# Attention with pairs weighted between scores and transposes, inverse sums spread by matmuls, and other steps for VectorE's copies

## What is computed

```python
q = _split_heads(query_antecedent @ Wq, h) * d_head ** (-0.5)
k = _split_heads(memory_antecedent @ Wk, h)
v = _split_heads(memory_antecedent @ Wv, h)
logits = jnp.einsum('bhqd,bhkd->bhqk', q, k) + bias
weights = jax.nn.softmax(logits, axis=-1)
x = jnp.einsum('bhqk,bhkd->bhqd', weights, v)
b, _, l, d = x.shape
x = x.transpose(0, 2, 1, 3).reshape(b, l, h * d)
return x @ Wo
```

## Time and profile before

| | us |
|---|---|
| median of the timed runs | 1054.37 |
| profiled execution | 1050.43 |
| its span, first to last instruction | 1048.7 |
| PE busy | 985.9 (94%) |
| VectorE busy | 611.1 (58%) |
| ScalarE busy | 484.5 (46%) |
| GpSimd busy | 261.3 (25%) |

### The profile page before, as it was taken

How to read it: one execution, slowest core, us unless ns; L and a number is a source line. 1 busy time by engine, 2 the same in 40 slices (tenths; PEclk the granted TensorE clock), 3 DMA queues, 4 the chain that set the end, 5 groups by cost and what they waited for, 6 DMA issues and landing times.

```text
span 1048.7 us, 17978 instructions
## 1 busy us (share of the span) xinstructions
PE 985.9 (94%) x7218; PEld 798.9 (76%) x7218; DVE 611.1 (58%) x1209; ACT 484.5 (46%) x625; POOL 261.3 (25%) x223
## 2 busy tenths in 40 slices
PE   7899999999999999999999999768869999999995
PEld 6588777888777888777887777343459999989884
DVE  4335986465986466986454984588961112455551
ACT  3111786062786155786151786368711102455551
POOL 0401840001840001840001830588310101111100
PEclk9999999999999999999999999898959999999998
DMA  8182871522871614871421853700059949699930
GB/s 281 40 156 76 191 185 47 203 81 75 192 180 47 264 40 151 191 175 50 150 106 37 195 124 122 283 1 2 23 189 389 377 164 342 206 381 334 329 91 13
DMA packets 76923, 169.91 MB, mean 162 GB/s; under 512 B 6440, under 2 KB 16808, under 8 KB 71968
## 3 DMA queue, kind: packets, MB, share of 16 engines
q1 hardware_dynamic: 74720, 163.87, 51.0%
q0 software_dynamic: 2112, 4.80, 2.0%
HBM read 119.01 MB, written 16.10 MB: 129 GB/s over the span
## 4 chain that ended last, share of the span: by engine, by line
PE 78%; DMA 6%; DVE 6%; POOL 4%; issue 3%; ACT 2%; SPq 1%; POOLq 0%; DVEq 0%; ACTq 0%
PE psum L461 11%; PE psum L2117 9%; PE psum L441 7%; PE psum L476 7%; PE psum L2132 6%; PE psum L380 5%; PE psum L397 5%; PE psum L398 5%; PE psum L399 5%; PE psum L381 5%; PE psum L382 5%; DMA xg<-xm_rows,row_id 3%; PE psum L2149 2%; PE psum L2151 2%; PE psum L2150 2%
## 5 line engine op out<-in xcount | busy, mean ns | idle before, releaser
L883 POOL CAST stack<-kT 128x2048 fp32r<-128x2048 f32 x32 | 64.0, 2006 | 405.3 <-DVE keys_lo L592 393.6
L628 DVE CUSTOM_DVE_ANT_0 prob<-psum,biasmap,top 128x512 f32<-128x512 f32 x192 | 144.2, 751 | 21.4 <-PE psum L441 12.0
L796 ACT ACTIVATE prob<-prob,top 128x2048 f32<-128x2048 f32 x64 | 128.5, 2008 | 27.0 <-DVE top L628 26.6
L461 PE MATMUL psum<-ident,prob 128*128 128x128 f32 x1024 | 134.9, 275 | 1.2 <-issue 0.8
L2117 PE MATMUL psum<-xT,wring 128*128 128x128 f32 (+3 forms) x1024 | 135.1, 293 | 0.6 <-ACT xT L2430 0.6
L2117 PEld LDWEIGHTS psum<-xT,wring 128*128 128x128 f32 x1024 | 132.7, 193 | 1.5 <-ACT xT L2430 0.8
L461 PEld LDWEIGHTS psum<-ident,prob 128*128 128x128 f32 x1024 | 116.3, 141 | 22.1 <-issue 7.5
L758 ACT COPY kT<-psum 128x512 f32<-128x512 f32 x64 | 37.5, 586 | 198.7 <-PE psum L382 191.7
L804 ACT COPY probT<-psum 128x1024 f32<-128x1024 f32 x96 | 96.5, 1010 | 45.6 <-PE psum L476 44.0
L397 PE MATMUL psum<-wv_hi,ctx_part 128*128 128x512 f32 x256 | 100.1, 391 | 0.0
L398 PE MATMUL psum<-wv_lo,ctx_part 128*128 128x512 f32 x256 | 99.8, 390 | 0.0
(11 more groups left out here) (256 smaller groups left out, 1721.1 us busy)
## 6 DMA issues: line engine op xcount, KB each, us to landing
wring<-in_w SPq DMA_DIRECT2D x64, 1024.0 KB, 7.8
ctx_raw<-in_ctx_t SPq DMA_DIRECT2D x15, 1024.0 KB, 6.0
stack<-stack SPq DMA_DIRECT2D x32, 256.0 KB, 4.7
early_stack<-early_stack SPq DMA_DIRECT2D x28, 256.0 KB, 5.2
ternary<-ternary_weights SPq DMA_DIRECT2D x1, 6272.0 KB, 24.7
prob<-in_w_gate_t SPq DMA_DIRECT2D x1, 5632.0 KB, 17.4
stack<-key_stack SPq DMA_DIRECT2D x20, 256.0 KB, 3.9
query_stacks<-prob SPq DMA_DIRECT2D x16, 256.0 KB, 5.4
```

What stands on the lines that cost most here:

```text
L461: mm = pe.transpose(psum[:, w + i, j * P:(j + 1) * P], prob[:, prob_slot(n, j), kt * P:(kt + 1) * P], ident[:, :])
L628: dve.tensor_tensor_reduce(prob[:, slot, keys], psum[:, scores.of[n, j, c], :], biasmap[:, keys], 1.0, top[:, h, (c + 1) % 2:(c + 1) % 2 + ...
L796: act.activation(prob[:, slot, :], prob[:, slot, :], ACT.Exp, bias=top[:, h, 1:2], scale=-1.0, accum_out=top[:, h, 2:3]).then_inc(*raised. ...
```

## The change

- In a slot, and in the tail, PE weighs the older pair first, then turns the sums where they are due, and then turns the newer pair. The first of these stood last before.
- The spread copy goes. `turn_sums` makes four matmuls, one for each head, with that head's column of `rinv` repeated 32 times as the weights and the identity as the moving operand; each writes its 32 rows of the bank. It waits for the reciprocal (`inverted`). `copy_sums` now has the wait for the `finish` before it, and the reciprocal a wait for the sums turned two quads before.
- VectorE's pairs are 2 and 6 where they were 3 and 7, and 2, 6 and 7 in the third quad where they were 3, 6 and 7.
- `finish` of the quad before the last stands between the two bias additions of slot 3; it stood behind both.

```diff
-MOVED_BY_VECTOR = ((3, 7), (3, 7), (3, 6, 7), (7,))
+MOVED_BY_VECTOR = ((2, 6), (2, 6), (2, 6, 7), (7,))
...
             def turn_sums(n):
                 w, free = scores.take(("sums", n), sums_copied.at(n))
-                pe.wait_ge(*spread_out.at(n))
+                pe.wait_ge(*inverted.at(n))
                 pe.wait_ge(*free)
-                pe.transpose(psum[:, w, 0:P], inverse[:, :], ident[:, :]).then_inc(*sums_turned.made(n))
-
-            def turn_and_weigh(b, turned_step, weighed_step):
+                for j in range(QUAD):
+                    mm = pe.matmul(psum[j * DH:(j + 1) * DH, w, 0:P], rinv[:, n % 2, j:j + 1].broadcast_to([P, DH]),
+                                   ident[:, :], start=True, stop=True, tile_position=(0, j * DH))
+                mm.then_inc(*sums_turned.made(n))
+
+            def weigh_and_turn(b, turned_step, weighed_step, summed):
+                if weighed_step is not None:
+                    multiply_pair(*pair_of_step(b, weighed_step))
+                if summed is not None:
+                    turn_sums(summed)
                 if turned_step is not None:
                     turn_pair(*pair_of_step(b, turned_step))
-                if weighed_step is not None:
-                    multiply_pair(*pair_of_step(b, weighed_step))
...
-            def spread_sums(n):
+            def invert_sums(n):
                 g = n % DT
                 dve.wait_ge(*raised.at(n, QUAD - 1))
-                dve.reciprocal(rinv[:, n % 2, :], top[:, QUAD * g:QUAD * (g + 1), 2]).then_inc(*own.made())
-                dve.wait_ge(*own.last())
+                if n >= 2:
+                    dve.wait_ge(*sums_turned.at(n - 2))
+                dve.reciprocal(rinv[:, n % 2, :], top[:, QUAD * g:QUAD * (g + 1), 2]).then_inc(*inverted.made(n))
+
+            def copy_sums(n):
+                dve.wait_ge(*sums_turned.at(n))
                 if n >= 1:
                     dve.wait_ge(*weighted.at(n - 1))
-                dve.tensor_copy(inverse[:, :].rearrange("p (j d) -> p j d", j=QUAD),
-                                rinv[:, n % 2, :].rearrange("p (j d) -> p j d", d=1).broadcast_to([P, QUAD, DH])
-                                ).then_inc(*spread_out.made(n))
-
-            def copy_sums(n):
-                dve.wait_ge(*sums_turned.at(n))
                 dve.tensor_copy(inverse[:, :], psum[:, scores.of["sums", n], 0:P]).then_inc(*sums_copied.made(n))
...
-                        for c in (2 * half, 2 * half + 1):
-                            add_bias(n, j, c)
+                        add_bias(n, j, 2 * half)
+                        if i == FINISH_AT and n > DT * b + 1:
+                            finish(n - 2)
+                        add_bias(n, j, 2 * half + 1)
                         step = steps_of_slot(n, i)[0] if n > DT * b else None
                         if step is not None and by_vector(*pair_of_step(b, step)):
                             move_pair(*pair_of_step(b, step))
-                        if i == 3 and n > DT * b + 1:
-                            finish(n - 2)
-                        if i == 3 and n > DT * b:
-                            spread_sums(n - 1)
+                        if i == INVERT_AT and n > DT * b:
+                            invert_sums(n - 1)
                         if i == SUMS_AT and n > DT * b:
                             copy_sums(n - 1)
```

More of the change, by code:

```diff
@@ L56 @@
 FILLERS = (2, 1, 2, 1, 2, 1, 2, 1, 2, 2)
-SUMS_AT = 5
+FINISH_AT, INVERT_AT, SUMS_AT = 3, 3, 5
 class Events:
@@ L290, in perceiver_block @@
         moved_a = events("moved_a", [(n, p) for n, p in pairs if not by_vector(n, p)])
-        spread_out = events("spread_out", quads)
-        sums_turned, sums_copied = events("sums_turned", quads), events("sums_copied", quads)
+        inverted, sums_turned, sums_copied = (events(name, quads) for name in ("inverted", "sums_turned", "sums_copied"))
         weighted = events("weighted", quads)
@@ L539, in tensor_attention @@
                         if n > DT * b:
-                            turn_and_weigh(b, *steps_of_slot(n, i))
-                        if n > DT * b and i == SUMS_AT:
-                            turn_sums(n - 1)
+                            weigh_and_turn(b, *steps_of_slot(n, i), n - 1 if i == SUMS_AT else None)
                 work.restart()
                 for t in TAIL:
-                    turn_and_weigh(b, t, t - WEIGH_LATER)
-                    if t == STEPS - 3:
-                        turn_sums(DT * (b + 1) - 1)
+                    weigh_and_turn(b, t, t - WEIGH_LATER, DT * (b + 1) - 1 if t == STEPS - 3 else None)
                 multiply_pair(*pair_of_step(b, STEPS - 2))
@@ L742, in vector_attention @@
                 finish(last - 1)
-                spread_sums(last)
+                invert_sums(last)
                 if b + 1 < B:
```

## The result

The changed kernel takes 1061.71 us (median of 10 runs, 1057.32 to 1065.23), the kernel before beside it 1054.03 (10 runs): ratio 1.0069, 95% interval 1.0051 to 1.0087, some 7.7 us more. The forecast was 1060.7 us and +6.3.

The account below looks back on a forecast made before the run. The prediction took PE to bound the attention slots. Its terms, -3.3 + 2.1 + 7.7 + 0.5 - 0.7 = +6.3 us, carried over to the timed median of 1054.37 gave 1060.7 us, own range 1057.5 to 1063.5.

Parts of the forecast that it names:

- The bound: Attention stage: PE's blocks follow without a gap, 2.11 us a slot, so only PE's blocks or waits count.
- Order: Attention slots on PE: scores (S) 0.63, weighting (W) 0.58, transposes (T) 0.85; slot 2.06 instead of 2.11 us, -3.3 us.
- Sums by matmuls: Inverse sums on PE: four matmuls, 0.22 us, replace one transpose; +2.1 us over the kernel.
- VectorE's steps: VectorE in attention: dropping the spread copy and moving `finish` and other waits costs or saves PE nothing, 0 us.
- Copies: VectorE's copy of pair 2 before slot 5's additions stalls slot 6's second score matmul 0.64 us, 12 times: +7.7 us.
- The 0.5 us for slot 2: Copy of pair 6 behind slot 0 delays slot 2's second score matmul by 0.06 us in 8 places: +0.5 us.
- the small gains: Shorter wait for ScalarE's first copy in quad 1's slot 4, and no last-exponential wait in the tail: -0.7 us together.
- A: Score ring: PE hides the stall, being held elsewhere by as much; 1055 us, or 1053.0 with no stall; chance 0.18.
- B: PE's attention slots: cheaper junctions between blocks give a slot of 1.92 us and a total of 1049.5 us; chance 0.12.
- C: PE's attention: first, the order saves nothing, 1064.0 us; second, the repeated column loads slowly, 1066.5; chance 0.12 for both.

## Why the prediction was right

Point by point, by its own steps.
- **The bound.** PE without a gap in the slots: right. Each edit showed up in the attention stretches through PE's blocks or PE's waits.
- **Order.** S 0.63, W 0.58, T 0.85, slot 2.06: measured 0.64 to 0.65, 0.57 to 0.58, 0.85, 2.07. Prices read from rows with the same neighbours carried over. Against the kernel before, the blocks S and T of the slots give 2.1 us, where I had 3.3: the 0.015 us by which S is longer than I took stand there some 80 times. The tail, which I put at nothing, takes 0.5 of it back: the order before ended in two weightings in a row, 1.01 us, and in the new order a turn stands between them and they take 0.57 or 0.58 each. The Trainium skill ("TensorEngine Tiling", Key Properties) says only that a change of tiling mode drains TensorE. Read as one price for every change, which is how I set it against my rows, it gives a slot of 2.11; the slot of 2.07 is against that reading, by 0.04 us a slot.
- **Sums by matmuls.** +2.1 us forecast, 2.0 to 2.1 measured in the blocks of the kernel with them alone, and 2.4 in the changed kernel, where the turn behind the sums lasts 0.88, 0.03 more than I took. In the changed kernel, though, this term isn't there to be added: PE would have waited for the same bank without it, as the run with the old transpose showed.
- **VectorE's steps.** 0 forecast, and no wait for `finish` and none behind pair 7 shows in the changed kernel. The order alone shows what the two edits kept away: 1.4 us and 4.4 us.
- **Copies.** Twelve stalls of 0.64 forecast, 7.7 us; twelve of 0.49 measured, 5.9 us. The mechanism was right and the size too large, by two latencies. A turn in front of S frees VectorE 0.28 us after the next slot starts (305.53 against 305.25), not 0.37; and PE's matmul starts 0.06 us after the bank is read out (308.27 against 308.21), not 0.17. PE also reaches the slot 0.04 later, after 2.32 us and not 2.28. The other way, the W behind a late matmul starts 0.43 after it (308.27 to 308.70), not 0.31. The 0.5 us for slot 2 weren't there: with the 0.28 the additions are in time.
- **The sum.** +6.3 forecast, +6.46 in the stretches, +7.7 in the medians. That the first two agree so well is luck in good part, as the copy terms were 2.3 too large together and the order 1.2 too favourable. The blocks of both timelines, one by one, divide the 6.46 so: stalls +5.9; sums +2.4; order in the slots -2.1; quad 1's slot 4 -0.7, where the turn behind ScalarE's first copy takes 0.85 for 1.02 (this and 0.2 in the tail are the small gains that I put at 0.7); a wait of 0.23 us that only before's trace has, -0.2; the tails without the sums +0.8, mainly the 0.5 just named, less 0.2, and 0.4 in the last batch with its wait for a DMA; the projections of quad 0 and of the first slots of quad 1 +0.3. Together +6.4. What makes the medians differ by 1.2 us more than the stretches isn't settled; the interval of the ratio (+5.4 to +9.2 us) takes in both.
- **Rivals.** A (hidden stall) is refuted by the twelve S of 1.13. B (cheaper junctions) is refuted by the blocks. C's first half is refuted by the slot of 2.07, its second by 0.22 to 0.25 us for the sums.
- **The range.** 1061.71 lies in the prediction's own range, 1057.5 to 1063.5. Its sentence that the range takes in A's 1053 and C's 1064.5 doesn't go with that range, and C's own sum was 1064.0.

What the prediction got right by its sum it described badly in one respect: it treated the parts as additive. The three parts alone cost 5.2 (order), 2.4 (matmuls) and 6.5 (copies) us of stretches, 14.1 together; the change, which is these three and the new place of `finish` (it has no run of its own), costs 6.5. The waits of the order alone go with pairs 3 and 7 and with the old place of `finish`, and the stall of the copies hides the matmuls.

## What to carry to other kernels

Where two engines hand banks round a ring, write down for each place when the reader is done and when the writer comes back, before moving any work in the reader's queue: a copy of 1.14 us placed ahead of two reads instead of behind them cost 0.49 us twelve times, while that reader was busy for only 58% of the span. A guest in the ring, here the sums, makes it one bank shorter just then, so put it where the reader is ahead. And test the parts of a combined change alone and the whole without each: here the parts didn't add, one constant (`SUMS_AT` 6 instead of 5) undid the loss, and the part that saved VectorE's copy, sixteen times 0.23 us, cost PE about 2 us, on the engine that was the bound.

## What the runs showed of the hardware

- A block's price depends on its neighbours: the eight transposes take 0.79 us from start to start between two score blocks, 0.96 between scores and a weighting, 0.85 the other way round (304.40 to 305.25 after the change) and 1.03 between two weightings. VectorE, which waits for the end of a turn, started 0.28 us after the start of the S behind it (305.53 against 305.25).
- Four matmuls with a column repeated 32 times as weights (a step of zero) cost no more than four weightings of the same shape: weighting and sums together are 24 instructions in 0.80 us, and 16 take 0.57.
- PE's granted clock averaged between 0.92 and 1.00 over the first 40 us in ten profiled executions, and the first score matmul, which the edits don't touch, came at 105.9 us in one with 1.00 and at 110.1 in the one with 0.92. Times of single runs of the kernel before scatter from 1050.3 to 1059.8 us. Each kernel has one profile here, so the scatter of the stretches isn't measured; some of them hold a single wait for a DMA, of 0.4 or 0.7 us.
